# A new order of one step's work on three engines, edges' one-hots ahead of scores, and the normalised rows of x moved to GpSimd for seven of twelve blocks

## What is computed

```python
h = relu(layernorm(x)); scores = h @ weight @ input.T          # 6144 x 6144
x = x + softmax(where(adj > 0, scores, -2**32+1) / 0.07) @ input
h = relu(layernorm(x)) @ W                                      # 6144 x 128
e = leaky_relu(h @ a_src + (h @ a_dst).T)
att = softmax(where(adj > 0, e, -1e9)), thresholded at 1e-4, times the row's number of edges
x = x + elu(h + att @ h)
```

## Time and profile before

| | |
|---|---|
| median of three executions | 653.78 us (652.53 to 654.51) |
| the profiled execution | 656.63 us, span of its trace 654.8 us |
| busy in the span | DVE 481.7 us, ACT 408.3, PE 399.8, POOL 299.5 |
| mean granted TensorE clock | 0.81 of full speed |
| moved | 186.78 MB, 285 GB/s over the span |

### The profile page before, as it was taken

The page is one execution under the profiler, slowest core; times in us unless marked ns, Lnnn a source line. Parts: engine busy times, 40 slices in busy tenths (PEclk is TensorE's granted clock), DMA queues, the critical chain, the costliest instruction groups (busy, mean ns, idle before and its releaser), DMA issues.

```text
span 654.8 us, 9849 instructions
## 1 busy us (share of the span) xinstructions
PE 399.8 (61%) x3012; PEld 274.8 (42%) x3043; DVE 481.7 (74%) x2172; ACT 408.3 (62%) x424; POOL 299.5 (46%) x335
## 2 busy tenths in 40 slices
PE   2465475767668696777677765866382521546654
PEld 0111233344436263544455443635271521546653
DVE  0176178798988798979898996979847413579994
ACT  3667778999999789979889979973221100022232
POOL 6001660515151332406076674747777767777000
PEclk9657577999998889978979998867856755657777
DMA  9999999999999999999999999942222232234222
GB/s 327 413 419 421 419 368 406 383 408 407 409 408 407 370 350 392 400 407 373 367 403 369 403 398 409 397 181 55 68 70 54 71 99 53 55 103 127 75 81 83
DMA packets 37767, 186.78 MB, mean 285 GB/s; under 512 B 7888, under 2 KB 8144, under 8 KB 18896
## 3 DMA queue, kind: packets, MB, share of 16 engines
q1 hardware_dynamic: 28496, 167.02, 64.8%
q0 software_dynamic: 9216, 19.11, 10.2%
HBM read 179.73 MB, written 6.37 MB: 284 GB/s over the span
## 4 chain that ended last, share of the span: by engine, by line
DVE 41%; DMA 14%; PE 12%; POOL 11%; issue 10%; ACT 10%; SPq 2%; DVEq 0%; ACTq 0%; POOLq 0%
DMA arena<-in_adj 13%; POOL arena L808 6%; ACT arena L862 6%; PE K L1424 4%; DVE keys L1018 3%; DVE G L1129 2%; ACT R_all L891 2%; POOL X L800 2%; DVE RTp L1188 2%; POOL arena L800 2%; DVE stats L1226 1%; POOL E L808 1%; PE G L1637 1%; DVE cand L1048 1%; DVE X L1368 1%
## 5 line engine op out<-in xcount | busy, mean ns | idle before, releaser
L862 ACT ACTIVATE arena<-arena,half_c 128x2048 fp8e4<-128x2048 int32 x144 | 283.7, 1999 | 38.0 <-DMA arena<-in_adj 35.9
L800 POOL DMA_INDIRECT X<-in_L_gnn_input,idx_all x132 | 125.8, 953 | 203.9 <-DVE idx_near L1100 167.0
L1424 PE MATMUL K<-arena,bits 128*128 128x512 fp8e4 x576 | 168.0, 431 | 47.4 <-DVE keys L1018 24.2
L808 POOL DMA_INDIRECT arena<-table,idx_near x96 | 92.5, 964 | 30.3 <-issue 29.0
L1424 PEld LDWEIGHTS K<-arena,bits 128*128 128x128 bf16 x576 | 58.9, 108 | 91.1 <-ACT arena L862 28.5
L1018 DVE MAX8 keys<-K 128x8 int32<-128x128 f32 x192 | 42.4, 281 | 41.4 <-PE K L1424 41.4
L808 POOL DMA_INDIRECT E<-table,idx_near x48 | 45.6, 949 | 14.6 <-issue 14.6
L1517 PE MATMUL W<-X,RTp 128*128 128x128 f32 x240 | 35.9, 289 | 4.6 <-DVE RTp L1188 3.5
L1436 PE MATMUL G<-g,R_all 128*128 128x128 bf16 x324 | 26.5, 234 | 19.8 <-DVE g L1151 14.3
L891 ACT CAST R_all<-G 128x512 fp8e4<-128x512 f32 x36 | 19.8, 585 | 28.4 <-remote 14.9
L824 POOL TENSOR_TENSOR E<-E 128x3072 f32<-128x3072 f32 (+3 forms) x4 | 12.9, 3223 | 51.4 <-DMA E<-in_L_gnn_input 51.2
(11 more groups left out here) (255 smaller groups left out, 988.0 us busy)
## 6 DMA issues: line engine op xcount, KB each, us to landing
arena<-in_adj SPq DMA_DIRECT2D x144, 1024.0 KB, 10.8
table<-hs SPq DMA_DIRECT2D x12, 262.0 KB, 10.0
hs<-table SPq DMA_DIRECT2D x12, 262.0 KB, 2.8
E<-in_L_gnn_input SPq DMA_DIRECT2D x3, 1024.0 KB, 15.0
out_x<-x_all SPq DMA_DIRECT2D x12, 256.0 KB, 2.0
x_all<-in_x SPq DMA_DIRECT2D x1, 2560.0 KB, 14.1
X<-in_L_gnn_input,idx_all POOLq DMA_INDIRECT x132, 6.2
arena<-table,idx_near POOLq DMA_INDIRECT x96, 2.5
```

Source lines behind the costliest of these rows:

```text
L800: pool.indirect_dma_start(out=x_of(b)[:, e, :], out_offset=None, in_=inp, in_offset=bass.IndirectOffsetOnAxis(ap=idx_all[:, at:at + 1], ax ...
L808: pool.indirect_dma_start(out=E[g][:, t, :], out_offset=None, in_=tables[g], in_offset=bass.IndirectOffsetOnAxis(ap=idx_near[:, t, g:g + 1 ...
L862: nc.scalar.activation(sign[:, load % RING, :], ring[:, load % RING, :], ACT.Sign, bias=half_c[:], scale=1.0, saturate=False).then_inc(sig ...
L1424: last = mm(bank_[:], bits[:, third * TB + j, :], sign[:, load % RING, j * FOLD:(j + 1) * FOLD], start=False, stop=(third == G - 1 and j = ...
```

## The change

It moves calls within a step on DVE, ACT and PE, and moves `hidden_x` of blocks 0 to 6 from ACT to POOL. A smaller edit takes one DVE instruction (`exp_i`) out of each of the three levels of `decode`. Waits are altered where the new order needs it: `edges_lists` instead of `first_edges` waits for the record of block b4, and `spread(b2)` waits for the one-hots of block b1.

```diff
+    X_BY_POOL = 7
@@ POOL
+                def hidden_x(b):
+                    pool.wait_ge(ln_x_r, (FROM[b] + SIZES[b] - 1) // PART + 1)
+                    wait(pool, hx_turned, b)
+                    for t in range(SIZES[b]):
+                        tile = FROM[b] + t
+                        last = pool.tensor_scalar(hx[:, t, :], x_all[:, tile, :], rstd_x[:, tile:tile + 1],
+                                                  shift_x[:, tile:tile + 1], ALU.mult, ALU.add)
+                    link(last)
+                    pool.tensor_scalar(hx[:], hx[:], 0.0, None, ALU.max).then_inc(hx_r, 1)
                 sum_of_input()
+                hidden_x(0)
                 for n in range(1, NB):
                     neighbours(n - 1, 0, BG)
+                    if n < X_BY_POOL:
+                        hidden_x(n)
@@ ACT: hidden_x(b) returns at once for b < X_BY_POOL; one step
+                    more(1)
                         exponent(b3)
                     more(1)
-                        hidden(b4)
+                        keep_turned(b4)
+                        keep_turned_x(b2)
                     more(2)
                         exponent_of_edges(b3)
-                        keep_turned(b4)
+                        keep_h(b4)
                     more(1)
-                        hidden_x(b1)
-                        keep_h(b4)
                         keep_high(b2)
-                    more(6)
+                    more(2)
                         keep_R(b1)
                     more(1)
                         keep_RT(b1)
-                        keep_turned_x(b1)
                     more(1)
+                        hidden_x(b1)
+                    more(3)
+                        hidden(b3)
@@ DVE: decode
-                        ts(exp_i[:, 0:w], code_f[:, 0:w].bitcast(I32), 23, None, ALU.logical_shift_right)
@@ DVE: one step
                         decode(b1)
-                        shares(b3)
+                        differences(b3)
                         list_columns(b1)
+                        spread_lists(b1)
+                        ends_of_rows(b1)
+                        shares(b3)
+                    find(n, 0)
                         record(b4)
-                        spread_lists(b1)
                         split_g(b2)
-                        ends_of_rows(b1)
-                        score(b2)
-                    find(n, 0)
-                        pieces_of_scores(b2)
+                        columns_of_edges(b1)
                     find(n, 1)
-                        columns_of_edges(b1)
+                        score(b2)
+                        pieces_of_scores(b2)
                         add_attention(b3)
-                        centre(b2)
                         norms(b3)
                     find(n, 2)
-                        normalise(b2)
+                        rows_without_edges(b2)
+                        centre(b2)
                     find(n, 3)
-                        rows_without_edges(b2)
-                        differences(b2)
+                        normalise(b2)
@@ PE: in spread(b, t)
-                    pe.wait_ge(RT_r, RPARTS[b + 1])
+                    pe.wait_ge(RT_r, RPARTS[min(b + 2, NB)])
@@ PE: in first_edges(b)
-                    wait(pe, rec_r, b - 2)
@@ PE: in edges_lists(b)
+                    wait(pe, rec_r, b - 2)
@@ PE: one step
-                        edge_shares(b3)
                     more(1)
+                        turn_hid(b4)
+                        edge_shares(b3)
+                    more(1)
                         project_hx(b2)
-                        turn_hid(b4)
-                    more(1)
                         project_hid(b4)
                     more(2)
-                        attend(b3)
                         first_edges(b1)
                     more(1)
-                        spread(b2, 0)
-                    more(1)
-                        spread(b2, 1)
-                        spread(b2, 2)
-                        spread(b2, 3)
-                    more(1)
                         make_R(b1)
-                        turn_hx(b1)
+                    more(1)
                         edges_lists(b1)
-                        rows(b2)
                         make_RT(b1)
-                    more(5)
+                        attend(b3)
+                    more(1)
+                        for t in range(SIZES[b2]):
+                            spread(b2, t)
+                    more(12)
+                        turn_hx(b1)
+                        rows(b2)
```

More of the change, by code:

```diff
@@ L503, in fast_path @@
         col_f = sb("col_f", [P, B * NKEY])
-        exp_i = sb("exp_i", [P, B * NKEY], I32)
         top_i = sb("top_i", [P, B * NKEY], I32)
@@ L865, in hidden_x @@
                 def hidden_x(b):
+                    if b < X_BY_POOL:
+                        return
                     act.wait_ge(ln_x_r, (FROM[b] + SIZES[b] - 1) // PART + 1)
@@ L944, in _ @@
                     if 0 <= b4 < NB:
-                        hidden(b4)
+                        keep_turned(b4)
+                    if 0 <= b2 < NB:
+                        keep_turned_x(b2)
                     more(2)
@@ L963, in _ @@
                         keep_RT(b1)
-                        keep_turned_x(b1)
                     more(1)
+                    if 0 <= b1 < NB:
+                        hidden_x(b1)
+                    more(3)
+                    if 0 <= b3 < NB:
+                        hidden(b3)
                     if n == 0:
@@ L1032, in decode @@
                     for level in range(LEVELS):
-                        ts(exp_i[:, 0:w], code_f[:, 0:w].bitcast(I32), 23, None, ALU.logical_shift_right)
                         link(ts(top_i[:, 0:w], code_f[:, 0:w].bitcast(I32), 0x7F800000, None, ALU.bitwise_and))
-                        stt(cand[:, 0:size, level, :], exp_i[:, 0:w].rearrange("p (b e) -> p b e", b=size), float(FOLD),
-                            col_f[:, 0:w].rearrange("p (b e) -> p b e", b=size), ALU.mult, ALU.add)
+                        stt(cand[:, 0:size, level, :], top_i[:, 0:w].rearrange("p (b e) -> p b e", b=size),
+                            float(FOLD) / (1 << 23), col_f[:, 0:w].rearrange("p (b e) -> p b e", b=size), ALU.mult, ALU.add)
                         link(tt(code_f[:, 0:w], code_f[:, 0:w], top_i[:, 0:w].bitcast(F32), ALU.subtract))
@@ L1247, in _ @@
                     if 0 <= b3 < NB:
-                        shares(b3)
+                        differences(b3)
                     if 0 <= b1 < NB:
                         list_columns(b1)
+                        spread_lists(b1)
+                        ends_of_rows(b1)
+                    if 0 <= b3 < NB:
+                        shares(b3)
+                    if n < NB:
+                        find(n, 0)
                     if 0 <= b4 < NB:
                         record(b4)
-                    if 0 <= b1 < NB:
-                        spread_lists(b1)
                     if 0 <= b2 < NB:
@@ L1452, in make_R @@
                     pe.wait_ge(below_r, b + 1)
-                    wait(pe, spread_used, FROM[b])
+                    if b > 0:
+                        wait(pe, spread_used, FROM[b - 1])
                     for i in range(0, SIZES[b] * G, 4):
@@ L1560, in more @@
                             fold(n, c)
+                    more(1)
+                    if 0 <= b4 < NB:
+                        turn_hid(b4)
                     if 0 <= b3 < NB:
@@ L1567, in _ @@
                     if 0 <= b4 < NB:
-                        turn_hid(b4)
-                    more(1)
-                    if 0 <= b4 < NB:
                         project_hid(b4)
                     more(2)
+                    if 0 <= b1 < NB:
+                        first_edges(b1)
+                    more(1)
+                    if 0 <= b1 < NB:
+                        make_R(b1)
+                    more(1)
+                    if 0 <= b1 < NB:
+                        edges_lists(b1)
+                        make_RT(b1)
                     if 0 <= b3 < NB:
@@ L1576, in _ @@
                         attend(b3)
-                    if 0 <= b1 < NB:
-                        first_edges(b1)
                     more(1)
                     if 0 <= b2 < NB:
-                        spread(b2, 0)
-                    more(1)
-                    if 0 <= b2 < NB:
-                        spread(b2, 1)
-                        spread(b2, 2)
-                        spread(b2, 3)
-                    more(1)
+                        for t in range(SIZES[b2]):
+                            spread(b2, t)
+                    more(12)
                     if 0 <= b1 < NB:
-                        make_R(b1)
                         turn_hx(b1)
-                        edges_lists(b1)
                     if 0 <= b2 < NB:
                         rows(b2)
-                    if 0 <= b1 < NB:
-                        make_RT(b1)
-                    more(5)
```

5 lines of the change are left out of this document (removed).

## The result

The changed kernel takes 674.23 us (median of 4, 669.28 to 682.76) against 654.14 before: a ratio of 1.028 [1.024, 1.032], slower by 20 us and outside the forecast range. The ratio leaves out the execution of 682.76, which lies over 1.5% above the fastest of the four. Its profiled execution took 672.0 us with a span of 670.3. The steps of the prediction are followed in these two profiled executions, 654.8 and 670.3 us of span.

The account below looks back on a forecast made before the run. DVE was taken to set the pace, with transfers close behind. Terms of -1 in steps 1 to 3, +7.9 in the steps and -6 in the tail gave +0.9 on the 653.78 median: 654.7 us, range 638 to 667.

Parts of the forecast that it names:

- The loop: Ring of waits through ACT, PE and DVE, from one step's norms to the next: a floor of 36.6 us a step.
- The loop isn't there: Rival: an order or wait was misread, steps fall to 34.1 us in practice, 636 us in all; chance 0.16.
- the short loop: Rival: steps of 36.1 us, full tail gain of 7 us, 649 us in all; chance 0.20.
- I take 36.8: Step length in us chosen for the seven steps from decode of step 4 to decode of step 11.
- the upper bound of 37.8: Longest step in us allowed for, if PE is at half clock for part of each.
- the working's 36.6: Sum in us a step of ACT 21.5, PE 5.9 and DVE 9.2, with PE at full clock.
- The term of +7.9: Cost in us of seven steps, from decode of step 4 to decode of step 11, at 36.8 instead of 35.7.
- PE's clock falls ahead of attend: Rival: PE stands still before c0, its clock drops, steps of 38.2 us, 664 us in all; chance 0.26.
- -1: Steps 1 to 3: a gain of 1 us (0 to 3), since block 0's lists come earlier.
- The tail: After decode of step 11: earlier gathers and score save 6 us, bounds 3 and 7.5.
- D + 20.3: Block 10's gathers start 20.3 us after decode of step 11 starts, 7.0 us earlier than before.
- its rival: POOL's 3.1 us of hidden_x arithmetic a block blocks DVE, 1.6 us more a step, 666 us; chance 0.07.

Follow-up runs that it names:

- spread_first: Changed kernel with attend(b3) behind spread(b2) on PE instead of ahead of c6: 652.26 us, ratio 0.997.
- the pads: Changed kernel with three extra ACT copies in steps 4 to 11: ahead of hidden, in ACT's idle time, 673.10 us; ahead of keep_R, in the loop, 692.25 us.
- x_on_act: Changed kernel with hidden_x of all twelve blocks back on ACT, behind keep_RT: 681.50 us, ratio 1.040.
- 11: Changed kernel with attend behind the spreads in all steps but the last decode step, and hidden_x of all blocks on ACT: 650.33 us, ratio 0.994.
- 7: Changed kernel with attend behind the spreads on PE in all steps but step 11, where it stays ahead: 650.47 us, ratio 0.996.
- run 4: Changed kernel with attend behind spread on PE, and loads c0 and c1 ahead of hidden on ACT: 652.22 us, ratio 0.997.

## Why the prediction was wrong

**The loop is there, and the whole loss hangs on it.** The prediction found norms, hidden, eight loads, keep_RT, attend, spread, score by reading three lists together. spread_first takes attend out of it and gains 22 us; the pads show that ACT's time counts in the loop and not ahead of hidden. What was to be seen was seen: DVE idle ahead of score for the spread (3.6 us in the turn shown), next to none ahead of columns_of_edges (0.54), ACT idle ahead of hidden (4.8 to 7.5 in steps 4 to 11, the longer ones while POOL has hidden_x). "The loop isn't there" falls, and so does the short loop.

**The step was mis-sized.** "I take 36.8" is the step that failed. Measured were 38.0, above even the upper bound of 37.8: the working's 36.6 plus 1.2 us in which keep_turned waits for turn_hid at half clock, which gives the 37.8 of a settled step, and step 4 of 39.5, of whose 1.7 us more its attend of 4.6 is 0.8. The term of +7.9 was +16.0. The rival "PE's clock falls ahead of attend" (38.2 a step, 664 us) had nearly the right step, with the fall where it put it, between rows(b2) and c0. But its price is paid ahead of turn_hid in every step, and in attend only in some. The prediction gave 26 in 100 to this and took the floor "with PE at full clock and nobody else late", though its own working showed PE standing still for 4 us in each step. The Trainium skill (TensorE: Matmul & The Clock Gate, "Why this matters for your kernels") warns of such gaps; the trace agrees for the stop of 6.0 us (clock 0.50), and of the stops of 3.0 in spread_first three of eight were followed by a fold at half clock.

**Steps 1 to 3 had the wrong sign.** "-1" was +3.4, 163.8 against 160.4. The lists do come earlier (decode of step 2 at 87.1 us against 95.5, of step 3 at 122.2 against 126.6), but "mostly wait for loads" overlooked that step 3 has norms(0) and attend(0), so the loop's first pass falls in it, with its loads late and attend 2.0 us longer.

**The tail gave 4.2 us, not 6.** neighbours(10) waits for attend as foreseen, but starts at D + 22.4, not D + 20.3: 1.2 is the wait for turn_hid, and 0.8 lies between the end of attend (451.16) and the first gather (451.94). Score(11) starts at D + 80.5, not 78. From there to the last third it takes 39.2 us, where the kernel before takes 39.8.

Summed in the profiled spans, against the forecast: 4.4 + 8.1 + 1.8 + 0.3 in the rest, 14.6 us, which is 670.3 less the 655.7 forecast. The spans differ by 15.5 us, the medians by 20.1. The other 4.6 are where the profiled executions lie: the one before 2.5 us above its median, the one after 2.2 below. Plain executions of the changed kernel lie between 669 and 683 us, both profiled ones (672.0 and 672.1) near their lower end, so what makes the longer ones long shows in no trace. That they are executions in which more attends fall at half clock, as in x_on_act, would fit, but isn't shown.

**hidden_x on POOL** was rightly costed at nothing (11 against 7). But the sign that the prediction gave for its rival is in the trace: POOL's arithmetic does hold DVE up. In the changed kernel it falls into decode.

```profile
163.56 1.87 POOL L811 TENSOR_SCALAR hx<-x_all,rstd_x,shift_x 128x128 f32<-128x128 f32 x4
```

The first cast of decode, shown above, took 0.56 us beside it in step 4 and 0.23 in step 11, where POOL does no arithmetic. All of decode up to the first MAX8 on cand took 5.2 us in steps 4, 6 and 7 against 3.7 in steps 8 to 11, and 3.7 in all of these steps in x_on_act. The Trainium skill (SBUF — State Buffer, "Who interferes with whom") has a lock on a port pair that the two share; the trace agrees in that DVE's instructions stretch, by 1.5 us of the 3.4 that hidden_x takes. The rival's price fails all the same: decode isn't in the loop, and DVE still waits 2.8 us or more for the spread in these steps. In the order of 7 the move costs nothing either. Luck has a part here: the prediction set the price at nothing for POOL's and ACT's spare time, and didn't work out where in DVE's step POOL's arithmetic would fall.

**Open:** why the second fall of the clock meets attend in every step of x_on_act and in few of the changed kernel, when the code of the later steps is the same; why a stop of 3.0 us is followed by the fall in some steps and not in others; and what holds the steps of run 4 at 35.4.

## What to carry to other kernels

In a software pipeline (steps that overlap, here with a list of calls for each engine), follow the lists as one ring across the steps: a call at the end of one list that waits for another engine's late result makes the length of the ring a floor for the step, and one call moved behind another on the third engine may lift it. Where such a ring makes an engine stand, add to its length what a fallen clock costs the first matmuls behind the stop, and take that as the likely case. A pad of known length, once inside the suspected ring and once beside it, tells whether it is there.

## What the runs showed of the hardware

- In a stop of 6.0 us on PE the granted clock fell to 0.50, and 4 fp8 matmuls of 128x512 took 1.91 us instead of 1.02. Behind eight stops of 3.0 us in spread_first they took 1.02 to 1.14 five times and 1.77 to 1.92 three times. In the changed kernel the clock was at 0.50 behind a stop of 3.2 us too (368 to 370).
- Six f32 matmuls, 2.3 to 2.7 us, in the stop of 6 us didn't bring the clock back for c0 in seven of eight steps; sixteen, 3.8 to 5.5 us, did in all.
- DVE's decode, up to its first MAX8 on cand, took 3.7 us with no more than the end of a gather on POOL beside it, and 5.2 beside POOL's tensor_scalar; a cast of 128x128 took 0.56 us instead of 0.23.
- POOL's tensor_scalar with two per-partition operands took 0.44 us for 128x128 f32, and the maximum of 128x512 took 1.50, where 1.3 was expected from 0.99 for 128x384.
